# A selective-scan layer and its coupling layer: the last coupling update moved into the token sum, GpSimd's products by a table, side work at other places

## The reference

```python
# layer 1 (selective scan), per sequence x[1024, 256]
xi, res = split(x @ W_in.T + b_in)              # 512 channels each
xi = silu(causal_conv4(xi) + b_conv)
delta = softplus(xi @ Wx_d.T + b_d);  B, C = xi @ Wx_bc.T + b_bc     # 16 states
h[t] = exp(delta[t] * A) * h[t-1] + delta[t] * B[t] * xi[t]          # per channel and state
y[t] = sum_states(h[t] * C[t]) + xi[t] * D
x1 = layernorm(x + (y * silu(res)) @ W_out.T + b_out)
# layer 2 (coupling), three cycles
g = sigmoid net of mean over tokens of x1       # once per sequence
o = x1
for _ in range(3):
    t = sigmoid net (4 layers, gelu) of o       # per token
    c = 0.1 + range * (0.7 * g + 0.3 * t - 0.5) * 2
    o = o + c * twist(o)                        # [o_r, o_i, p_r, p_i] -> [p_r, -p_i, -o_r, o_i]
out = layernorm(x1 + o)
```

## Time and profile before

| | us |
|---|---|
| median of three runs | 4091.69 |
| the profiled execution | 4096.96 |
| its span, first to last instruction | 4095.2 |
| GpSimd busy | 3645.5 (89%) |
| VectorE busy | 3565.9 (87%) |
| TensorE busy | 3478.7 (85%) |
| ScalarE busy | 2757.6 (67%) |
| DMA, share of 16 engines | 46% |

### The profile page before, as it was taken

The page is one execution under the profiler, slowest core; times in us unless marked ns, Lnnn a source line. Parts: engine busy times, 40 slices in busy tenths (PEclk is TensorE's granted clock), DMA queues, the critical chain, the costliest instruction groups (busy, mean ns, idle before and its releaser), DMA issues.

```text
span 4095.2 us, 50321 instructions
## 1 busy us (share of the span) xinstructions
PE 3478.7 (85%) x18264; PEld 1585.3 (39%) x18264; DVE 3565.9 (87%) x2796; ACT 2757.6 (67%) x3278; POOL 3645.5 (89%) x1604
## 2 busy tenths in 40 slices
PE   7678989898898889989898998888989898897665
PEld 3224343343434334343443434334343443434232
DVE  3989898999889999898998989999999998989871
ACT  4556858677685866848677684866858577684742
POOL 4998989989898998989999998998989999898961
PEclk9779999999998999989899999999999999998878
DMA  4454372544546454363644546354363544436230
GB/s 175 135 186 132 118 238 94 202 149 140 181 139 197 139 182 142 122 226 105 201 138 150 171 139 207 129 194 144 116 219 120 192 139 168 149 124 225 101 101 26
DMA packets 329125, 629.88 MB, mean 154 GB/s; under 512 B 27440, under 2 KB 226096, under 8 KB 328624
## 3 DMA queue, kind: packets, MB, share of 16 engines
q1 hardware_dynamic: 328880, 626.67, 46.1%
HBM read 456.70 MB, written 169.87 MB: 153 GB/s over the span
## 4 chain that ended last, share of the span: by engine, by line
POOL 51%; DVE 15%; issue 12%; PE 9%; ACT 7%; DMA 6%; SPq 1%; DVEq 0%; POOLq 0%; ACTq 0%
POOL work L1055 30%; POOL work L1062 14%; DVE da L975 8%; DMA c_quad<-bc_scratch 3%; PE banks L608 3%; POOL oT L1071 3%; POOL oT L1070 3%; POOL soft L1077 2%; DVE work L975 2%; ACT L745 2%; DVE work L983 2%; PE banks L629 2%; ACT da L798 1%; DMA u_q<-u_scratch 1%; DMA u_scratch<-soft 1%
## 5 line engine op out<-in xcount | busy, mean ns | idle before, releaser
L1055 POOL TENSOR_TENSOR work<-u_q,b_quad 128x1024 f32<-128x1024 f32 x1024 | 2398.5, 2372 | 126.0 <-DMA u_q<-u_scratch 104.5
L975 DVE TENSOR_TENSOR_SCAN da<-da,work 128x1024 f32<-128x1024 f32 x640 | 1462.7, 2285 | 188.1 <-ACT da L798 131.9
L798 ACT ACTIVATE da<-delta_q,neg_a 128x1024 f32<-128x1024 f32 x1024 | 1128.1, 1112 | 679.2 <-DVE work L983 470.1
L1062 POOL TENSOR_TENSOR work<-work,c_quad 128x1024 f32<-128x1024 f32 x384 | 909.1, 2368 | 75.7 <-DVE work L975 75.1
L720 PE MATMUL y_sum<-work,v_all 128*32 128x256 f32 x8192 | 627.5, 414 | 380.8 <-POOL work L1062 232.5
L975 DVE TENSOR_TENSOR_SCAN work<-da,work 128x1024 f32<-128x1024 f32 x384 | 865.7, 2275 | 39.9 <-ACT da L798 39.0
L983 DVE TENSOR_TENSOR work<-da,c_quad 128x1024 f32<-128x1024 f32 x640 | 781.8, 1222 | 41.9 <-DMA c_quad<-bc_scratch 21.0
L745 ACT ACT_TABLE_LOAD x563 | 722.3, 1283 | 14.7 <-DMA v_all<-in_vectors 3.7
L720 PEld LDWEIGHTS y_sum<-work,v_all 128*32 128x32 f32 x8192 | 213.4, 113 | 822.9 <-POOL work L1062 291.2
L608 PE MATMUL banks<-xi,w_all 128*128 128x512 f32 x1024 | 476.0, 608 | 7.4 <-ACT big L769 4.7
L595 PE MATMUL banks<-xi,taps 128*128 128x512 f32 x984 | 446.2, 601 | 0.0
(11 more groups left out here) (81 smaller groups left out, 3156.5 us busy)
## 6 DMA issues: line engine op xcount, KB each, us to landing
delta_q<-delta_scratch SPq DMA_DIRECT2D x256, 512.0 KB, 4.6
u_q<-u_scratch SPq DMA_DIRECT2D x256, 512.0 KB, 6.3
delta_scratch<-delta SPq DMA_DIRECT2D x64, 512.0 KB, 2.8
u_scratch<-soft SPq DMA_DIRECT2D x64, 512.0 KB, 3.0
b_quad<-bc_scratch SPq DMA_DIRECT2D x64, 512.0 KB, 6.1
c_quad<-bc_scratch SPq DMA_DIRECT2D x64, 512.0 KB, 7.9
s_quad<-res_scratch SPq DMA_DIRECT2D x128, 256.0 KB, 4.5
y_scratch<-s_quad SPq DMA_DIRECT2D x128, 256.0 KB, 4.3
```

The source lines that it names most:

```text
L798: act.activation(da[:, t % 2, :], delta_q[:, slot, :], ACT.Exp, scale=neg_a[:, t % PERIOD:t % PERIOD + 1]).then_inc(da_ready, 1)
L975: dve.tensor_tensor_scan(dst, da[:, t % 2, :], work[:, slot, :], 0.0, ALU.mult, ALU.add) \
L1055: pool.tensor_tensor(work[:, slot, :], u_q[:, copied, :], b_quad[:, j, :], ALU.mult) \
L1062: pool.tensor_tensor(work[:, un % WORK, :], work[:, un % WORK, :], c_quad[:, un % PHASE, :], ALU.mult) \
```

## The change

Four things. (1) The third update is not made. The final sum takes it on TensorE: besides x1 and the transposes of oT it adds the transposes of big, the second with a negative unit matrix (minus, 64 KB more of vectors). It waits for the product of its half (f_prod) and not for updated. As big is then read, the residual x1 is loaded into the yg buffers (RES_IN_AT 28), and the final normalisation writes to oT, whose rows go out with four stores in place of two; x of the next sequence is loaded into oT only when these have landed (XRES_AT 66). (2) GpSimd takes 26 of 64 products by a table; TensorE sums one of them two units later or at its phase's last unit, whichever is first. (3) U_LAG is 6, O_STATS, O_RS, O_NORM 3, 5, 4. (4) Nearly all tables of places have other numbers.

```diff
-POOL_UNITS = ((1,), (0, 1))
+POOL_AT = (1, 4, 6, 8, 9, 10, 11, 12, 16, 18, 21, 24, 28, 32, 33, 36, 42, 44, 49, 52, 55, 56, 58, 59, 60, 61)
-X_AT = (0, 0, 20, 24, 37, 39, 45, 47)
-V_AT = (2, 5, 28, 28, 41, 41, 51, 53)
-RES_AT = (0, 0, 26, 27, 37, 39, 48, 50)
+X_AT = (0, 0, 19, 24, 37, 37, 45, 49)
+V_AT = (2, 3, 27, 29, 41, 41, 53, 52)
+RES_AT = (0, 1, 26, 26, 36, 39, 47, 50)
-O_AT = (5, 7, 10, 12)
-T_AT = (13, 14, 15, 15)
+O_AT = (5, 9, 10, 12)
+T_AT = (15, 15, 15, 15)
-F_AT = (-1, 0, 2, 2, 4, 4, 6, 8, 10, 10)
-G_AT = (17, 18, 22)
-E_AT = (59, 61, 61, 62)
+F_AT = (-1, 0, 1, 2, 4, 5, 6, 9, 10, 10)
+G_AT = (16, 19, 21)
+E_AT = (57, 58, 59, 61)
-DELTA_TAKE, DELTA_MAX, U_LAG = 3, 3, 7
-O_STATS, O_RS, O_NORM = 2, 3, 3
+DELTA_TAKE, DELTA_MAX, U_LAG = 3, 3, 6
+O_STATS, O_RS, O_NORM = 3, 5, 4
-DST_AT, UST_AT = (8, 3, 3, 9), (9, 4, 8, 10)
-DLD_AT, ULD_AT = (10, 12, 11, 18), (11, 13, 13, 16)
-SLD, YST = 0, 0
-YGLD_AT = (1, 2, 5, 7)
-RESST_AT = (4, 36, 46, 54)
-X1ST_AT = (12, 13)
-RELOAD_AT, XRES_AT = 52, 63
-OUT_AT = (65, 66)
+DST_AT, UST_AT = (7, 5, 10, 8), (11, 5, 8, 9)
+DLD_AT, ULD_AT = (12, 13, 18, 19), (12, 13, 17, 20)
+SLD, YST = -1, 0
+YGLD_AT = (2, 4, 4, 8)
+RESST_AT = (4, 28, 47, 61)
+X1ST_AT = (15, 16)
+RES_IN_AT = 28
+XRES_AT = 66
+OUT_AT = (64, 64)
-BCST_AT = 49
-LB_AT, LC_AT = (52, 55, 59, 60), (60, 62, 63, 62)
+BCST_AT = 54
+LB_AT, LC_AT = (59, 55, 57, 63), (61, 62, 61, 63)
...
 def by_pool(u):
-    return u % PHASE in POOL_UNITS[(u // PHASE) % 2]
+    return u % PERIOD in POOL_AT
 def reduced_at(t):
-    units = []
-    late = t - REDUCE_LAG
-    if late >= 0 and late // PHASE == t // PHASE and by_pool(late):
-        units.append(late)
-    if not by_pool(t):
-        units.append(t)
-    return units
+    first, last = t - t % PHASE, t - t % PHASE + PHASE - 1
+    return [u for u in range(first, t + 1) if t == (min(u + REDUCE_LAG, last) if by_pool(u) else u)]
...
-                if (f := batch_at(t - PERIOD, RELOAD_AT)) is not None:
+                if (f := batch_at(t - PERIOD, RES_IN_AT)) is not None:
                     for h in range(2):
                         sp.wait_ge(x1_stored[h], 16 * (f + 1))
-                    sp.wait_ge(updated, CYCLES * f + CYCLES)
-                    sp.dma_start(x1, x1_dram[f].rearrange("(k p) c -> p k c", p=P)).then_inc(re_in, 16)
+                    sp.wait_ge(o_ready, 4 * f + 4)
+                    sp.dma_start(residual, x1_dram[f].rearrange("(k p) c -> p k c", p=P)).then_inc(re_in, 16)
...
                     if f:
-                        sp.wait_ge(e_ready, 4 * f)
+                        for h in range(2):
+                            sp.wait_ge(out_done[h], 32 * f)
                     sp.dma_start(x_res, x[f].rearrange("(k p) c -> p k c", p=P)).then_inc(xr_in, 16)
...
                 elif kind == "e":
-                    pe.wait_ge(updated, CYCLES * f + CYCLES)
                     pe.wait_ge(re_in, 16 * (f + 1))
+                    pe.wait_ge(f_prod, 2 * (CYCLES * f + CYCLES - 1) + n // 2 + 1)
...
-                        pe.matmul(half, eye, x1[:, tb, :], start=True, stop=False)
+                        pe.matmul(half, eye, residual[:, tb, :], start=True, stop=False)
                         for m in range(2):
-                            mm = pe.matmul(half[:, m * P:m * P + P], oT[:, m, tb * P:tb * P + P], eye,
+                            pe.matmul(half[:, m * P:m * P + P], oT[:, m, tokens], eye, start=False, stop=False)
+                            mm = pe.matmul(half[:, m * P:m * P + P], big[:, 1 - m, tokens], minus if m else eye,
                                            start=False, stop=m == 1)
...
-                    for c in range(CYCLES):
+                    for c in range(CYCLES - 1):
                         if pos == CYCLE_AT[c] + UPD_AT:
```

26 lines of the change are left out of this document (15 added, 11 removed).

## The result

| | before | after |
|---|---|---|
| median of the runs, us | 4092.68 (4090.53 to 4094.01) | 4049.49 (4047.96 to 4055.52) |
| ratio, 95% interval | | 0.9898 [0.9881, 0.9915] |
| the profiled execution, its span | 4096.96, 4095.2 | 4055.52, 4053.7 |
| first scan | 64.9 | 62.9 |
| period 0 | 226.7 | 225.1 |

The lower five lines are worked out from the starts of VectorE's scans in the two timelines (a period runs from its scan of unit 0 to the next one). The span is 41.5 us shorter: 14 x 2.32 = 32.5 in the periods, 3.6 in the last one, 1.8 in the tail, 2.0 before the first scan, 1.6 in period 0. Forecast were 98, 5, 8, 0 and 0. So the sign was right and the size was not: 43 us of 111. Two thirds of what was forecast is missing, and nearly all of it in the 14 periods.

A forecast was written before the change was run, and what follows sets the result against it. No engine bounds the 244.7 us period alone; its quarters (16 units each) become 62.9, 58.4, 58.3 and 58.6, taken as 7.0 us saved a period. Periods -98, last period -5, tail -8: -111, giving 3980 us, range 3900 to 4055.

The forecast's parts named there:

- The bound: Whole period of 244.7 us: GpSimd works 227.3, VectorE 221.8, TensorE 216.2; no engine bounds it alone, they take turns.
- Work and its places: Units 0 to 15: VectorE's busy time falls from 61.0 to 55.9 us; GpSimd's operations take 60.3 there.
- b_quad: At unit 3, before dbx 3: GpSimd idles 2.6 us a period, between 0 and 6, for row group 3's load.
- u_q: Before dbx 0: four GpSimd operations cover most of the u chain; 0.6 us of the wait for its load stays.
- ScalarE's detours: At ScalarE's function table changes for gates and gelu: VectorE's waits fall from 12 us a period to 8.
- Its waits for products are order waits: TensorE's sums of units 9 to 11 stand behind GpSimd's step 14; costed at nothing, with 17.9 us of idle cover.
- The gates at units 24 and 32 wait less: VectorE's gates at these units: 2.2 us less waiting, as GpSimd's last unit before 32 is 28, not 29.
- the seam: Where one period meets the next: VectorE's wait, 4.1 us in the period shown, becomes about 1.
- Rival (b): VectorE's waits all stay, elsewhere in the period: 242.3 us a period, 4048 in all; chance 0.21.
- Rival (c): TensorE's waits all stay and 3.6 us of work come on top: 248.3 us a period, 4134 in all; chance 0.07.
- x's load: Into oT once the output has landed, wanted at unit 5: cost 0, at most 5 us a period.
- First and last period, tail: First period 0; last period -5 us, between 0 and -9; the end after the last coupling product net -8.

The follow-up runs named there:

- the three moves: The changed kernel with b_quad's group 3 loaded early, x loaded in two halves and x_feat's load at place 52: 4000.4 us, 0.9777.

## Why the prediction was off, by its steps

**The bound.** "Nobody bounds it alone, the engines take turns" holds: GpSimd 227.5 of 242.4, and the experiments that lighten TensorE or ScalarE gain less than they take away.

**Work and its places.** Right: VectorE's busy time by quarter 55.9, 54.9, 54.0, 55.6 for 55.9, 54.5, 53.8, 55.3. Quarter 1 went from VectorE's pace to GpSimd's; 62.6 for 62.9. GpSimd alone takes 2.34 us for an operation of this size and 2.367 in the mean of the stretch, 2.370 before: beside VectorE's operations with an operand in PSUM it loses 0.03 us. The Trainium skill, "SBUF — State Buffer", section "SBUF: two separate sides", has among the conditions of its lock a VectorE operation with two SBUF inputs; the trace agrees in so far as VectorE's scans and products, each with an input in PSUM, did not hold GpSimd up.

**b_quad.** Forecast 2.6 us a period, measured 1.8 (GpSimd's idle time before dbx 3, mean of periods 1 to 14), and shown to count by taking it away: 26 us.

**u_q.** Forecast: 0.6 us before dbx 0. It is 2.1 in the mean where 4.5 stood, 2.7 a period stand before unit 56 and 1.8 before unit 36, so the whole wait hardly fell (98.0 to 93.2). Little of this counts: with x_feat at 52 the wait at unit 56 is gone and the period is 0.1 us shorter.

**ScalarE's detours.** From 12.9 us a period (exp 11.1, soft 1.7) to 9.7 (7.5, 2.2), forecast 12 to 8. The wait at unit 9 is gone, as said. The size is near; what it is worth was not. Taking all detours away turned 81 us of VectorE's waits into 39 of time, so a microsecond here is worth about half.

**The steps that failed.** The mechanism was not right in quarters 2 to 4. First, of TensorE: "Its waits for products are order waits", and "I cost them at nothing". That they are waits in order is so, but VectorE then waits for TensorE: in quarters 2 to 4 5.0 us a period (gates 2.6, factors 1.9, statistics of the final sum 0.5), forecast 0, before 2.2. In the whole period it is 10.3 for 5.1. Second, "The gates at units 24 and 32 wait less (GpSimd's last unit before 32 is 28, not 29): 2.2 less." The gate at 24 needs the product of unit 21, the same as in the old units, so it had no reason to; it waits 1.17 us for 1.04, the one at 32 1.35 for 1.15. GpSimd's last product is done 7.6 and 6.7 us before these gates start, VectorE's 3.7 and 3.6, and TensorE has side work in hand, as the rows of the gate at 24 show. That is one of the prediction's own signs of being wrong: "if a gate waits for it with GpSimd long done". Another sign missed is "TensorE idle near 18": it is 22.8. Third, the seam. The forecast took 3.1 us off VectorE's wait there, from 4.1 to 1, but 4.1 was the wait of the one period in the earlier trace rows; the mean of 14 is 1.8. The wait did go (0.2 is left), and brought 1.6.

The sum, from VectorE's row: in quarters 2 to 4 it idles 15.3 us where the forecast had 11.7, works 1.0 more, and quarter 1 is 0.3 shorter. That is the 4.2 by which the forecast's 238.2 falls short of 242.4. The levels came out nearer than the changes behind them. The period in the earlier trace rows had 66.3 us in quarter 1 and 62.3 in quarter 4, the mean has 67.5 and 59.8. So quarter 1 gained 4.9 where 3.4 was forecast, and quarter 4 gained 0.3 where 3.7 was: that its length was forecast within 0.9 is in part luck.

**Result by rival.** Rival (b), "VectorE keeps all its waits, elsewhere", gave 4048, and its premise holds to 1 us: 22.9 a period became 22.0. The forecast's sum had 18.7. That the total comes within 2 us is luck in part: VectorE's work is 1.0 over the rival's, its idle time 0.9 under, and the tail gave 1.8 for 8. Its mechanism was left open there; the runs show an exchange of waits between ScalarE, GpSimd and TensorE's order. Rival (c), in which TensorE's added work comes on top, is not what happened (-3.5 us for the new products, -8 for three taps, -16 on the kernel without table changes and with the three moves). The gates at 24 and 32 are held by TensorE's side work, as the rows show, but what moving that work would give was not tried, nor was the release of TensorE's three banks or delta's chain from unit 26 to u at 28; no run moves these one by one, so what closes the ring in quarters 2 to 4 stays open.

**x's load.** Forecast 0, at most 5: in the changed kernel TensorE waits 1.1 us a period for it, but 10 us where the final sum and the normalisations stand as before. So the forecast's 0 to 5 held for the whole change. Why the new places bear the late load and the old ones do not was not taken apart.

**First and last period, tail.** First scan 2.0 earlier and period 0 1.6 shorter, both forecast at 0; last period -3.6 for -5. Other runs with the changed kernel's preparation and units have the first scan at 62.8 to 64.4 and period 0 at 225.6 to 229.6, so little of these two gains is sure. From the last coupling product to the end it is 18.4 us where 28.8 stood (4066.40 to 4095.2 in the earlier trace rows), -10.4 for -8. The final sum starts at 4036.65, 0.14 us after the end of the product's first half (4036.51), as forecast:

```profile
3917.70 2.27 DVE L980 TENSOR_TENSOR_SCAN da<-da,work 128x1024 f32<-128x1024 f32 x1
...
3928.67 0.39 SPq L513 DMA_DIRECT2D oT<-in_x  x1
...
3935.36 3.47 PE L632 MATMUL banks<-w_all,yg 128*128 128x256 f32 x8 [13.44 <-DMA oT<-in_x]
...
3962.06 5.40 PE L679 MATMUL banks<-oT,w_all 128*128 128x512 f32 x8 [0.34 <-ACT oT L813]
...
4035.28 2.36 DVE L1007 TENSOR_TENSOR big<-banks,oT 128x1024 f32<-128x1024 f32 x2 [22.67 <-PE banks L701]
4036.65 0.67 PE L663 MATMUL banks<-yg,v_all 128*128 128x256 f32 x2 [1.28 <-DVE big L1007]
```

But from the last scan to that product it is 117.6 us where 109.05 stood, 8.5 more, which the forecast did not have: x is loaded only at 3928.67, behind the output, and the projection starts 17.7 us behind the last scan, 12.9 before; the first coupling cycle, from the first transposes (L640, 3957.66; 3992.42 before) to its product (3984.13; 4014.95), takes 26.5 us for 22.5. Of the tail's 8 us 1.8 are left. x in halves shortens it by 1.5 to 5.7.

## What to carry to other kernels

Where several in-order engines take turns, a wait taken off one engine's row is worth its time only in a stretch where that engine, or the one that it holds up, is busy throughout; elsewhere ask for each wait what is late next and by how much; here such waits gave back between nothing and half. Take what a wait can give from the mean of many periods, not from the one that is shown. For each engine that works through a list in order, look which side work stands before a result that another engine needs. A load moved in the queue that issues all transfers must be read with everything queued behind it: one position of one load was worth 26 us here, more than half of what the whole change brought. And two parts of a change can each cost 2% alone and be part of a gain together, so their prices on the kernel before do not add.
